# Three groups of list products, six one-hot rows on GpSimd, and shorter unread warm-ups in a two-layer transformer kernel

## The reference, cut to what matters

```python
scores = (jnp.tanh(xf @ gate_w.T) + 1.0) * 0.5        # 4096 tokens x 8 experts
vals, idx = jax.lax.top_k(scores.T, k)                # k = 512 tokens for each expert
y = _layernorm(xf[flat_idx].reshape(k, n, d), ln_gamma, ln_beta)
h = jax.nn.gelu(jnp.einsum('knd,nfd->knf', y, fc1s) + b1s, approximate=True)
o = (jnp.einsum('knf,ndf->knd', h, fc2s) + b2s) * kept_w[:, :, None]
out = xf.at[flat_idx].add(o.reshape(k * n, d))
```

## Time and profile before

| | us |
|---|---|
| three runs | 838.75, 835.82, 835.96 |
| median | 835.96 |
| profiled execution | 836.0 |
| its span, from the first to the last instruction | 834.3 |
| mean granted TensorE clock | 0.911 |
| PE, DVE, ACT, POOL busy | 671.5, 530.8, 454.9, 417.5 |

### The profile page before, as it was taken

How to read it: one execution, slowest core, us unless ns; L and a number is a source line. 1 busy time by engine, 2 the same in 40 slices (tenths; PEclk the granted TensorE clock), 3 DMA queues, 4 the chain that set the end, 5 groups by cost and what they waited for, 6 DMA issues and landing times. The chain is left out here.

```text
span 834.3 us, 18363 instructions
## 1 busy us (share of the span) xinstructions
PE 671.5 (80%) x6613; PEld 422.6 (51%) x6613; DVE 530.8 (64%) x1558; ACT 454.9 (55%) x696; POOL 417.5 (50%) x669
## 2 busy tenths in 40 slices
PE   8867999999778899999998959999996435987500
PEld 5433555555445556656665636666664213564400
DVE  6885888888467897788777833545456883222115
ACT  5535777777755466676665637676762540322102
POOL 5755777777630222242232226666664504788734
PEclk9986999999979999999999978999998757999655
DMA  4874553431000021372122137787751071444354
GB/s 163 259 226 117 163 153 90 122 89 43 3 2 1 0 58 39 95 190 58 38 58 77 57 95 171 189 197 180 199 133 54 6 207 28 98 103 99 36 95 125
DMA packets 104778, 85.83 MB, mean 103 GB/s; under 512 B 11760, under 2 KB 95216, under 8 KB 104560
## 3 DMA queue, kind: packets, MB, share of 16 engines
q1 hardware_dynamic: 97904, 79.34, 34.9%
q0 software_dynamic: 5632, 4.33, 3.7%
q10 hardware_dynamic: 1152, 0.98, 0.4%
HBM read 54.73 MB, written 29.49 MB: 101 GB/s over the span
## 5 line engine op out<-in xcount | busy, mean ns | idle before, releaser
L2216 ACT ACTIVATE a_prob<-a_ps_pair 128x1024 f32<-128x1024 f32 x96 | 93.1, 1023 | 48.0 <-PE a_ps_pair L2052 36.2
L1820 ACT ACTIVATE a_prob<-a_ps_pair 128x1024 f32<-128x1024 f32 x96 | 96.5, 1023 | 16.3 <-PE a_ps_pair L1526 13.4
L744 POOL TENSOR_TENSOR m_parts<-m_resid,m_parts 128x512 bf16<-128x512 f32 x32 | 37.8, 1183 | 130.3 <-ACT m_parts L637 130.3
L2228 POOL TENSOR_SCALAR_AFFINE_SELECT a_prob<-a_prob 128x512 f32<-128x512 f32 (+1 forms) x96 | 76.5, 804 | 51.0 <-ACT a_prob L2216 50.9
L1901 POOL TENSOR_SCALAR_AFFINE_SELECT a_prob<-a_prob 128x512 f32<-128x512 f32 (+1 forms) x96 | 75.4, 787 | 44.8 <-ACT a_prob L1820 44.1
L1711 DVE TENSOR_REDUCE a_mx<-a_ps_pair 128x4 f32<-128x1024 f32 x64 | 77.9, 1220 | 22.2 <-PE a_ps_pair L1571 20.5
L318 PEld LDWEIGHTS m_ps_n<-wd,m_act 128*128 128x128 f32 x512 | 66.7, 192 | 31.6 <-issue 31.3
L480 DVE SCALAR_TENSOR_TENSOR xn<-m_ps_n,m_wt,xn 128x128 f32<-128x128 f32 x256 | 71.7, 342 | 0.2 <-DVE xn L480 0.2
L318 PE MATMUL m_ps_n<-wd,m_act 128*128 128x128 f32 x512 | 67.7, 275 | 2.5 <-DVE xn L480 2.4
L306 PE MATMUL m_ps_u<-m_x1T,wgu 128*128 128x512 f32 x128 | 67.7, 611 | 0.0
L308 PE MATMUL m_ps_g<-m_x1T,wgu 128*128 128x512 f32 x128 | 66.1, 598 | 0.0
(11 more groups left out here) (314 smaller groups left out, 1534.6 us busy)
## 6 DMA issues: line engine op xcount, KB each, us to landing
qst<-scratch_q SPq DMA_DIRECT2D x64, 128.0 KB, 3.1
kst<-scratch_k SPq DMA_DIRECT2D x64, 128.0 KB, 3.2
scratch_q<-m_parts SPq DMA_DIRECT2D x32, 192.0 KB, 2.3
scratch_k<-m_parts SPq DMA_DIRECT2D x32, 192.0 KB, 2.3
qst<-scratch_q SPq DMA_DIRECT2D x32, 192.0 KB, 3.0
kst<-scratch_k SPq DMA_DIRECT2D x32, 192.0 KB, 3.6
c_w<-in_w SPq DMA_DIRECT2D x8, 578.0 KB, 4.0
scratch_q<-a_parts SPq DMA_DIRECT2D x16, 256.0 KB, 2.6
```

The lines of the kernel that those rows point to most:

```text
L1820: nc.scalar.activation(prob[:, r % 6, :], pair[(0, 2, 1)[j]][:, :], ACT.Exp, scale=scale, bias=0.0).then_inc(s_e, 1)
L2216: nc.scalar.activation(prob[:, r % 6, :], pair[r % 2][:, :], ACT.Square, scale=scale, bias=1.0).then_inc(s_e, 1)
L2228: nc.gpsimd.affine_select(out=blk, in_=blk, compare_op=ALU.is_ge, fill=0.0, base=0, pattern=[[0, n], [1, P]], channel_multiplier=-1).then_ ...
```

## The change

WARM goes from (13, 4, 6) to (6, 4, 3): six unread products at the start and three ahead of the list products. The 32 low rows are used in three parts, low rows 0 to 5, 6 to 15 and 16 to 31, with 48, 80 and 128 moving columns; the third result lies in the PSUM bank `ps_x[1]`, and the step behind waits for three parts. The last six of the 16 high rows are made by GpSimd, with the same instruction, and no longer by the vector engine. The semaphore that vector gives after `high` is now one of its own (`s_high`), for which GpSimd waits ahead of its six rows and vector ahead of its ten. TensorE waits for all six GpSimd rows ahead of each part.

```diff
-WARM = (13, 4, 6)
-HOT_PARTS = ((0, 10), (10, SLOTB))
+WARM = (6, 4, 3)
+HOT_PARTS = ((0, 6), (6, 16), (16, SLOTB))
+HOT_POOL = 6
...
-        found = (ps_l, ps_c)
+        found = (ps_l, ps_c, ps_x[1])
...
                 for half, (b0, b1) in enumerate(HOT_PARTS):
-                    pe.wait_ge(s_hot, SLOTA + b1)
+                    pe.wait_ge(s_hot, SLOTA - HOT_POOL + b1)
+                    pe.wait_ge(s_hotp, HOT_POOL)
...
-                pe.wait_ge(s_rows, 2)
+                pe.wait_ge(s_rows, len(HOT_PARTS))
...
-                v.tensor_tensor(high[:, :], whole[:, :], part[:, :], ALU.subtract).then_inc(s_st, 1)
-                done[0] += 1
+                v.tensor_tensor(high[:, :], whole[:, :], part[:, :], ALU.subtract).then_inc(s_high, 1)
                 step(v.tensor_copy(low[:, :], part[:, :]))
-                for i in range(SLOTA):
+                ve.wait_ge(s_high, 1)
+                for i in range(SLOTA - HOT_POOL):
...
+                pool.wait_ge(s_high, 1)
+                for i in range(SLOTA - HOT_POOL, SLOTA):
+                    nc.gpsimd.tensor_scalar(hot_a[:, :, i, :], high[:, :].rearrange("p (t e) -> p t e", e=E), float(SLOTB * i), row[:, 0:1],
+                                            ALU.is_equal, ALU.mult).then_inc(s_hotp, 1)
                 pool.wait_ge(s_d, 16)
                 pool.wait_ge(s_end, 1)
```

More of the change, by code:

```diff
@@ L883, in finish_layer1 @@
         s_hot = sem("onehots_ready")
+        s_high = sem("rank_high_ready")
+        s_hotp = sem("high_found_by_pool")
         s_l = sem("rows_found")
```

## The result

| | before | after |
|---|---|---|
| median | 836.23 us (833.7 to 838.75) | 838.65 us (835.78 to 840.36) |
| profiled execution | 836.0, span 834.3 | 835.9, span 834.2 |
| ratio to before | | 1.0027, 95% interval 1.0017 to 1.0038 |

The medians are of 19 runs each. One run of the changed kernel took 1645.42, twice the others, and nothing on record says why; the ratio and the range leave it out, and without it the median is 838.49. The change costs 2.3 us (1.4 to 3.2). That is inside the 0.5% which the prediction counted as the same, but on the other side of zero than the forecast of 835.0, and 0.2 to 0.4 above the upper end of its range, 838.3.

A forecast was written before the change was run, and what follows sets the result against it. It took a chain of work with no engine full as the bound, TensorE's unread work holding back the list products. Start +0.3, list stretch -2.0, last vector steps -0.1, expert 0 +0.8: -1.0 from 836.0, forecast 835.0, range 833.2 to 838.3.

The forecast's parts named there:

- What bounds the kernel: Whole kernel: a chain with no engine full; TensorE's own unread work holds the first list part back by 2.4 us.
- High rows on GpSimd: Last stage: six GpSimd rows at 0.77 us each end at 689.8, so list products begin at 690.0, not 692.37.
- Three list parts: List products: three parts take 3.9 us against 3.6, ending at 693.9 against 695.96, so -2.0 us.
- The unread products: Ahead of the list products, 6 to 3: six records end at 689.4 instead of 692.37, 2.9 us earlier.
- The start: Unread products at the start, 13 to 6: read work starts earlier but at the lower clock, +0.3 us.
- What the earlier indices meet: Expert 0's products: starting 1.7 us sooner with the clock rise unmoved, they lose time at the first scatter, +0.8 us.
- Low clock: Rival, list products: they run at the low clock; 835.9 if it rises at 693, 837.5 if never; chance 0.20.
- The engines in each other's way: Rival, high and low rows: vector rows stand still for each GpSimd row, giving 840.3; chance 0.10.
- Tipped clock: Rival, first attention: the early shift tips the clock into a low stretch there, giving 837.8; chance 0.12.
- All goes well: Rival, whole kernel: start -0.6, GpSimd row 0.65 (-2.7), clock rise moves along, giving 832.6; chance 0.08.
- the -3.3: List stretch: the best bound of the -2.0 us gain, with the cheap GpSimd row.

The follow-up runs named there:

- e3: The kernel before with three unread products ahead of the list products instead of six, nothing else: 839.06 us, 1.001 of before.
- e8: The kernel before with fifteen extra unread GpSimd instructions in five forms after high, while the vector engine waits: 852.45 us, one run.
- e12: The changed kernel with eight unread products ahead of the list products instead of three: 838.6 us, 1.0011 of before.
- e7: The changed kernel with six unread products ahead of the list products instead of three: 837.34 us, 1.0027 of before.
- e9: The kernel of e1 with list parts of 12, 12 and 8 low rows: 835.81 us, 0.9988 of before.
- e1: The changed kernel with all 16 high rows back on the vector engine: 834.97 us, 0.9973 of before.
- e6: The kernel before with only the six high rows moved to GpSimd: 839.1 us, 1.0050 of before, six runs.
- e2: The kernel before with six unread products at the start instead of 13: 836.43 us, 0.9988 of before.

## Why the prediction was wrong

**What bounds the kernel: right.** TensorE's own unread work held the first part back by 2.4: e3 takes three products away and the first list product comes 2.3 earlier.

**High rows on GpSimd: the step that failed.** 0.77 was taken for a row, with bounds of 0.60 and 0.96, and the row took 1.36, 1.23 of it with no neighbour. All of it came from rows on 128 columns of f32 and a slope of 0.114 per 128 columns from a masking instruction. e8 shows two terms mis-sized: the step from that form to 256 bf16 columns is 0.32, and the second operation, for which with the short runs 0.06 was allowed (0.77 - 0.71), is 0.22. With 0.60 + 0.32 + 0.22 = 1.14 the rows end at 685.2 + 6.8 = 692.0, and "the products begin at 690.0" becomes 692.2, almost no gain. The 0.09 from 1.14 to 1.23 are the gaps between the rows, the 0.13 to 1.36 the vector engine beside them. The prediction had the point right from which the step is worthless ("rows over 1.1"), but its bounds for a row ended at 0.96. The Trainium skill ("GPSIMD Engine Reference", 4.1 Engine selection) calls an instruction with one input "roughly line-rate" against the vector engine. The trace does not agree: 1.23 against 0.196 is six times.

**Three list parts: the second term.** 3.9 was forecast and 5.3 measured. In e12, with the clock up, the first two parts take 0.80 and 1.14 from start to start, and the last, at the upper level in both kernels, 1.80 in the chain of the changed one: 3.7 in all, so the prices stood (0.9, 1.15 and 1.8), and 48 columns lie near the line through the columns. What failed is that they would run at the upper clock: behind a wait of 3.8 us the first two did not. The cause lies in the first term, since the forecast had a wait of 0.6 (689.4 to 690.0).

**The unread products.** Their count was right only for products that start when they end. e7 and e12 show what it takes with dear GpSimd rows, e3 with large parts.

**The start: wrong sign.** +0.3 was taken, and 0.9 to 1.3 were won at that place, though no total shows them. 8.6 for the first vector step, the prediction's number for four records of 0.85, was met at 8.63, in part by luck: the records started 0.98, 0.85, 0.85 and 0.47 apart, and 0.43 from there on, so the clock rose at about 7.9. All eight took 5.04 and ended at 10.2, which is the better of the two cases in the text (10.3, with a rise at 8.6); the +0.3 leaned on the other (11.5, with a rise at 11), and in the quickest profile the eight took only 3.75.

**What the earlier indices meet: right in size, its reason not.** 0.8 of 1.7 was to be lost; e9 lost 0.8 of 1.9, e1 0.4 of 1.15. But the loss goes with the time from the start of expert 0's products to the rise of the clock, and this is not long because the products start early. It was 3.4 before, 4.7 in e1 and 5.2 in e9; it was also 5.2 in e6 and 5.4 in e3, whose indices come 1.2 *later* than before, and they too lost some 0.7 on the way to the first scatter. What sets it isn't shown by any run. In the changed kernel it was 4.1, and the first scatter lost 0.2 more.

**The rivals.** *Low clock* named what happened second, and its price for a clock that never rises, 837.5, is near the measured 838.65, but by another road: three unread products did raise the clock, and it fell in the wait. By its own terms that price should be 838.0 (836.0 + 1.8 + 0.3 - 0.1). *The engines in each other's way* happened in part: 1.8 us on the vector rows, where a stop for each row is 8.1, hidden behind GpSimd's, and 0.8 on GpSimd's own. The last low row came 8.3 behind `high` (684.91 + 5.81 - 682.41), short of the 9.0 (694.1 - 685.08) from which that rival decides. *Tipped clock* is seen in the changed kernel's own profile, at 50 us, but in kernels with thirteen unread products too, so it isn't the early start that tips it, and what it costs in the medians isn't known. *All goes well* and the -3.3 were out of reach: the third part waits for the last low row, by the forecast's own numbers at 691.7, and 691.7 + 1.8 = 693.5 leaves at most 2.4. In e1 the third part does wait for it.

With each term as measured the forecast's sum is: start -0.9, list stretch with the last vector steps +2.7, expert 0 +0.2, together +2.0; measured were +2.3 (1.4 to 3.2). The agreement is loose evidence, since the start's 0.9 is a mean over profiles that no total confirms.

## What to carry to other kernels

Price an instruction on another engine by its whole form, its columns, type, number of operations and kind of scalar; where the trace has none like it, the range must reach to the ratio of the two engines' nearest like rows, not to a slope from another kind of instruction. When part of a row of equal pieces goes to a slower engine, work out first how many it can finish before the earliest reader wants them: here three are in time and six are not, and even three gained nothing over none. Unread work that keeps TensorE's clock up is worth its time only if real work follows it soon, so it has to be fitted anew whenever what it covers moves.

## What the runs showed of the hardware

- A GpSimd instruction with one scalar operand on 256 bf16 columns takes 0.85 us, one that reads it per partition 0.92, with a second operation 1.07 to 1.15; runs of 8 cost the same as dense columns. The vector engine does the dearest of these in 0.196.
- Beside six such GpSimd rows 42 quick vector rows took 1.8 us longer and GpSimd 0.77. The vector engine was held up twice for each GpSimd row, by 0.13 and 0.20, and ran at its usual pace between; neither engine stood still for the other's whole instruction.
- TensorE's clock rose at 687.2 when the engine had just gone idle, and fell at 690.6 in the same idle time; a wait of 1.66 before the second part of e3 ended in a fall, the 1.24 of e6 did not.
- Small products lose less than half of their speed when the clock halves: 48 columns take 0.80/32 = 0.025 us in e12 and 1.27/32 = 0.040 in the changed kernel, 80 columns 1.14/32 = 0.036 and 2.05/32 = 0.064.
- From the start of expert 0's products to the rise of the clock it was 3.2 us (e2) to 5.4 (e3) over the fourteen profiles, and the first scatter came 12.8 to 13.7 behind that start: the later the rise, the later the scatter.
- The same start takes from 7.36 to 8.63 us to the first vector step: that is over a microsecond between executions, half of what this whole change costs, by when the clock rises.
